# A graph layer on one core: VectorE's masks and one-hots made one slot ahead, with other ring sizes

## The chip, the core and the metric

One core of a Trainium2 chip. The metric is the device time of one execution in microseconds; the kernel before takes 1254.35 us (median of 3 runs, 1250.93 to 1255.43). Smaller is better.

## What is computed

One layer of a graph network over 6250 nodes of 128 features and 200000 edges that are sorted by their destination:

```python
h = relu(layernorm(x))
H = gelu(h @ W1.T + b1)                       # 6250 x 128
T = gelu(H @ WA.T) @ WB.T                     # 6250 x 4, the mix weights of a node
agg = gelu(segment_sum(H[src][:, :, None] * T[src][:, None, :], dst))   # 6250 x 128 x 4
cnt, sT = segment_sum(1, dst), segment_sum(T[src], dst)
node = einsum('nhm,nm->nh', agg, sT) / max(cnt, 1)
out = x + gelu(concat([node, H])) @ W2.T + b2
```

The destinations are drawn unevenly: the low-numbered nodes have most of the edges.

## The kernel before

The sum over the edges is done in two ways side by side.

*Gathered part (nodes from 1536 on).* 796 tiles of 128 edges, in 398 groups of two. For each tile GpSimd gathers the 128 source rows (128 features, 4 mix weights and their bf16 parts) from `node_table` in HBM into a `ring` of 10 rows of tiles, one indirect DMA a tile (line 778, in program order, held at line 777 until the group that last used the ring slot is summed). VectorE makes a mask for the group: `make_eq` (L1158, two groups at a time) compares the destinations with 24 consecutive nodes, `make_mask` (L1170) multiplies with the four mix weights. TensorE sums the group with four matmuls over the masks and two over `eq` (`sum_group`, L1518 and L1521) into one of two pairs of PSUM halves; VectorE adds the result into the accumulator at a column that it reads into a register (`add_group`, L1182).

*Dense part (nodes up to 1535).* For these the kernel counts how often each source node sends to each destination node, and multiplies the count matrix with the products. The destinations fall into six chunks, treated one after the other from the last; a chunk's counts are made while the chunk before is multiplied. Per tile of edges ScalarE makes a one-hot of the source's low bits (L894 and L897, four tiles in a batch, two batches), VectorE a one-hot of the rest (`hots`, L1204, 294 to 490 columns, in `hot_a` with 6 buffers), and TensorE multiplies them (L1546). One to four tiles are a count group; its sum lies in one of two PSUM banks, and VectorE adds it into the count matrix (`add_counts`, L1195). The multiplication has 49 units a chunk, one for each 128 source nodes: 12 matmuls with the counts (L1565) and two or four for the sums (L1570). Each unit needs a 388 KB slice of `product_parts` from HBM, loaded by SyncE (L599) into one of 4 buffers (`cbuf`).

*Order.* Python lays out a list of slots ahead of time, `SLOTS`: 50 slots in stage 0, in which the `product_parts` are made (two slots for each pair of node tiles: L914 and L953 on ScalarE, L1325 and L1333 on VectorE, L588 the store), and 49 in each of the stages 1 to 5, one for each unit. A slot holds some groups of gathers and some count groups:

```
stage                      0    1    2    3    4    5
groups of gathers         50   52   76   78   78   64
count groups              76   50   81   92  112    0
tiles counted             76  100  210  228  234    0
slots with 3 count groups  0    0    0    4   24    0
```

Every engine walks the same list. TensorE does in each slot the sums of the slot's gathers, then its counts, then the unit. VectorE does for each group its mask, and after every second one the additions of the two groups before; then for each count group the one-hots and after them the addition of the count group before (`pending_c`), and in stage 0 its part of the products. At a stage's end ScalarE moves four PSUM banks out (`evacuate`, L903 and L905), and VectorE reads a maximum from what it moved (L1286). In stage 5 VectorE also checks counts and bounds, and SyncE loads some large arrays (`own_part`, `dense_columns`) in the same queue as the `product_parts`. A prologue of 84 us (the node table) comes before, and a tail of 58 us (the output) after.

What holds what back: a mask waits for its two gathers, and for the mask buffer of four groups before. A one-hot waits until the tile of `HA` before is counted. A group's sum waits for its mask, and the first of each pair for the additions of the pair before the last. A count group waits for its one-hots on both sides, and for the addition of the count group two before. A `product_parts` load waits for the end of the unit `CB` before.

## Time and profile before

```
median without a profile      1254.35 us (1250.93 to 1255.43)
span of the profiled run      1435.7 us
VectorE busy                   915.1 us (64%)
TensorE matmul busy           1168.7 us (81%)
GpSimd busy                    849.4 us (59%), nearly all gathers
ScalarE busy                   635.0 us (44%)
TensorE's granted clock        0.847 of full speed on average
```

All rows and durations below are from the one profiled execution. Its span is 181 us longer than the median of the runs without a profile, so a sum that is made in it has to be carried over. A granted clock of 1 means TensorE's level of 2.4 GHz all the time, 0.5 that of 1.2 GHz. The busy time of TensorE counts pipelined matmuls with modelled ends, so it isn't work alone. In the rows of waits, "issue" is idle time for which the profile shows no releaser, and "remote" a releaser that it has no record of; some matmul records are missing.

### The profile page before, as it was taken

The numbers are of one execution on the slowest core, as the hardware profiler recorded it, in microseconds if no ns is written. First come the engines' busy times: TensorE is split into PE (matmuls) and PEld (weight loads), VectorE is DVE, ScalarE is ACT, GpSimd is POOL, SyncE is SP. The second block draws the span as 40 slices with busy tenths as digits, with TensorE's granted clock in tenths as the row PEclk, the third lists the DMA queues.
The fourth block names the chain that finished last, engine by engine and source line by source line (L and its number), as shares of the span: only waits on it lengthen the run. The fifth ranks groups of instructions, "written<-read, shape, count | busy, mean of one in ns | idle before, by whom it ended". The sixth has DMA issues, their size and how long they took to land.

```text
span 1435.7 us, 26415 instructions
## 1 busy us (share of the span) xinstructions
PE 1168.7 (81%) x7416; PEld 773.5 (54%) x7416; DVE 915.1 (64%) x2876; ACT 635.0 (44%) x1498; POOL 849.4 (59%) x910
## 2 busy tenths in 40 slices
PE   5948777688887888988788888777888878779888
PEld 3724333366665555656556556555556655456544
DVE  8569987746764677675567767466666755262256
ACT  6976656344342455453455555244554531000023
POOL 5457655556566666666656566655655666656526
PEclk9965555589999999899989999988888999889978
DMA  6345544466555445444545444444444446765523
GB/s 203 130 135 175 171 145 161 142 184 180 167 169 165 134 135 135 126 138 138 144 123 137 121 123 133 140 129 120 127 121 109 125 127 185 176 186 169 174 47 84
DMA packets 100422, 205.73 MB, mean 143 GB/s; under 512 B 29570, under 2 KB 48336, under 8 KB 99611
## 3 DMA queue, kind: packets, MB, share of 16 engines
q1 hardware_dynamic: 74804, 146.92, 33.9%
q0 software_dynamic: 25472, 57.11, 16.2%
q8 instruction: 62, 1.02, 0.3%
q14 instruction: 84, 0.69, 0.1%
HBM read 171.73 MB, written 32.22 MB: 142 GB/s over the span
## 4 chain that ended last, share of the span: by engine, by line
PE 56%; DVE 15%; issue 14%; another core or an unknown queue 5%; DVEq 4%; ACT 3%; POOL 2%; DMA 2%; SPq 0%; ACTq 0%; POOLq 0%
PE ps L1565 23%; PE ps L1546 12%; PE ps L1518 12%; PE ps L1521 3%; DVE big L1195 3%; DVE big L1325 3%; DVE mask L1170 2%; PE ps L1570 2%; DVE q L1204 2%; DVEq L1152 2%; DVE big L1182 2%; POOL q L778 1%; DMA q<-node_table,src_g 1%; PE ps L1614 1%
## 5 line engine op out<-in xcount | busy, mean ns | idle before, releaser
L778 POOL DMA_INDIRECT q<-node_table,src_g x796 | 778.1, 977 | 497.1 <-PE ps L1521 218.6
L1565 PE MATMUL ps<-big,q 128*128 128x298 bf16 (+2 forms) x2940 | 522.7, 319 | 21.1 <-issue 14.2
L894 ACT ACTIVATE hot_b<-iota_b,q 128x128 bf16<-128x128 bf16 x848 | 270.0, 389 | 420.3 <-PE ps L1546 329.4
L1518 PE MATMUL ps<-mask,q 128*128 128x96 f32 x1592 | 291.2, 311 | 107.0 <-DVE mask L1170 67.8
L1565 PEld LDWEIGHTS ps<-big,q 128*128 128x128 bf16 x2940 | 286.5, 105 | 123.7 <-issue 31.1
L1195 DVE TENSOR_TENSOR big<-big,ps 128x294 f32 (+2 forms) x411 | 226.5, 551 | 186.4 <-PE ps L1546 125.6
L1518 PEld LDWEIGHTS ps<-mask,q 128*128 128x128 f32 x1592 | 244.9, 216 | 184.7 <-DVE mask L1170 118.3
L1546 PE MATMUL ps<-q,hot_b 128*128 128x294 bf16 (+2 forms) x848 | 221.7, 349 | 101.0 <-issue 58.4
L1204 DVE TENSOR_SCALAR q<-iota_a,q 128x294 bf16<-128x294 f16 (+2 forms) x848 | 238.0, 324 | 35.4 <-issue 19.8
L1170 DVE TENSOR_TENSOR mask<-eq,q 128x192 f32<-128x192 bf16 x398 | 141.9, 357 | 74.5 <-issue 40.0
L1182 DVE TENSOR_TENSOR big<-big,ps 128x120 f32 x398 | 110.2, 277 | 123.2 <-remote 53.0
L1546 PEld LDWEIGHTS ps<-q,hot_b 128*128 128x128 bf16 x848 | 73.7, 99 | 190.5 <-issue 85.6
L897 ACT ACTIVATE hot_b<-hot_b,ones 128x512 bf16<-128x512 bf16 x212 | 153.0, 722 | 6.9
L1570 PE MATMUL ps<-big,q 128*128 128x149 bf16 (+2 forms) x588 | 138.6, 236 | 3.2 <-issue 3.2
L1521 PE MATMUL ps<-eq,q 128*13 128x24 bf16 x796 | 82.4, 177 | 4.3 <-issue 4.3
L903 ACT ACTIVATE big<-ps 128x400 f32<-128x400 f32 x4 | 1.9, 484 | 188.9 <-PE ps L1565 188.9
L1570 PEld LDWEIGHTS ps<-big,q 128*128 128x128 bf16 x588 | 62.3, 106 | 40.8 <-issue 12.9
L1526 PE MATMUL ps<-zero 128*128 128x512 bf16 x126 | 69.7, 634 | 0.0
L914 ACT ACTIVATE big<-big 128x128 bf16<-128x128 f32 x196 | 59.7, 388 | 13.8 <-DMA big<-node_table 13.5
L1521 PEld LDWEIGHTS ps<-eq,q 128*13 128x13 bf16 x796 | 39.1, 88 | 46.8 <-issue 17.0
L1158 DVE TENSOR_TENSOR eq<-iota_b,dloc_g 128x96 bf16<-128x96 bf16 x199 | 51.1, 257 | 13.1 <-issue 3.3
L811 POOL TENSOR_TENSOR big<-big 128x1024 f32<-128x1024 f32 (+1 forms) x13 | 32.7, 2522 | 37.3 <-DVE big L1444 37.0
(145 smaller groups left out, 665.7 us busy)
## 6 DMA issues: line engine op xcount, KB each, us to landing
q<-product_parts SPq DMA_DIRECT2D x245, 388.0 KB
product_parts<-big SPq DMA_DIRECT2D x24, 776.0 KB
q<-node_table,src_g POOLq DMA_INDIRECT x796
node_table<-big SPq DMA_DIRECT2D x12, 280.0 KB, 3.0
big<-node_table SPq DMA_DIRECT2D x24, 140.0 KB
own_part<-big SPq DMA_DIRECT2D x12, 256.0 KB, 3.0
out_dram<-q SPq DMA_DIRECT2D x12, 256.0 KB, 2.0
big<-own_part SPq DMA_DIRECT2D x2, 1024.0 KB, 6.2
```

Source lines behind the costliest of these rows:

```text
L778: pool.indirect_dma_start(out=ring[:, t % R, :], out_offset=None, in_=table, in_offset=bass.IndirectOffsetOnAxis(ap=src_g[:, t:t + 1], axi ...
L894: last = nc.scalar.activation(hot_b[:, b % 2, i, :], iota_b[:, :], ACT.Abs, bias=nkey_b[:, t:t + 1])
L897: nc.scalar.activation(hot_b[:, b % 2, 0:n, :], hot_b[:, b % 2, 0:n, :], ACT.Relu, bias=ones[:, :], scale=-1.0).then_inc(hot_b_ready, 1)
L1170: nc.vector.tensor_tensor(mask[:, g % MB, :, :, :], eq[:, g % EB, :, None, :].to_broadcast([P, G, MIX, W]), ring[:, s:s + G, D:D + MIX][:, ...
L1182: nc.vector.tensor_tensor(to, to, group_psum(g, 0, SLOT) .rearrange("p (m w) -> p m w", w=W), ALU.add).then_inc(added, 1)
L1195: nc.vector.tensor_tensor(to, to, ps[:, 1 + c.number % 2, 0:NT * w].rearrange("p (a w) -> p a w", w=w), ALU.add).then_inc(counts_added, 1)
L1204: nc.vector.tensor_scalar(hot_a[:, ct % HA, 0:n], iota_a[:, 0:n], key_a[:, c.key + t:c.key + t + 1], None, ALU.is_equal).then_inc(hot_a_re ...
L1518: nc.tensor.matmul(o[:, 0:MIX * W], ring[:, s + t, 0:D], mask[:, b, t, :, :], start=(t == 0), stop=(t == G - 1))
L1521: last = nc.tensor.matmul(o[0:NP, MIX * W:SLOT], ring_b[:, s + t, TP:TP + NP], eq[:, e, t, :], start=(t == 0), stop=(t == G - 1))
L1546: nc.tensor.matmul(ps[:, 1 + c.number % 2, 0:n], hot_b[:, ct // HB % 2, ct % HB, :], hot_a[:, ct % HA, 0:n], start=(t == 0), stop=(t == c. ...
L1565: last = nc.tensor.matmul(ps[:, 3 + m, 0:n], c[:, LEAD + P * (MIX * part + m):LEAD + P * (MIX * part + m + 1)], counts[k % 2][:, a, c0:c1] ...
L1570: nc.tensor.matmul(ps[:, 3 + m, n:n + d1 - d0], c[:, 0:P], counts[k % 2][:, a, c0 + d0:c0 + d1], start=False, stop=False)
```

## The change

VectorE's loop over the slots is put in another order, and three sizes change.

- `prepare(slot)` is new. It does for every group of gathers of a slot the register load, `make_eq` and `make_mask`, and for every count group the wait for the keys, the register load and `hots`. It is called for the first slot ahead of the loop, and in each slot for the next one.
- In slot i, after `prepare(SLOTS[i + 1])`, come the additions of slot i: of gathers in pairs as soon as two are there, of all its count groups. `pending_c` is gone.
- VectorE's registers for start columns become 8 and 8 (6 and 4 before).
- `R`, the ring of gathers, 12 for 10; `HA`, VectorE's one-hot buffers, 8 for 6; `CB`, the `product_parts` buffers, 3 for 4.

No instruction on any engine is added or left out. The orders on TensorE, ScalarE, GpSimd and SyncE stay.

```diff
-R = 10
+R = 12
-HA = 6
+HA = 8
-CB = 4
+CB = 3
-        QW = 3104 + R * ROW + CTT + ...
+        QW = CB * CROW // 2 + R * ROW + CTT + ...
+            def prepare(slot):
+                for g in slot.gathers:
+                    starts_g[g] = column(regs_g[g % 8], base_g[:, g:g + 1], N - D0)
+                    if g % 2 == 1 and g + 1 < NG:
+                        make_eq(g + 1)
+                    make_mask(g)
+                for c in slot.counts:
+                    if c.index == 0:
+                        v.wait_ge(keys_ready, KEYED[c.chunk])
+                    cell = GROUP0[c.chunk] + c.index
+                    starts_c[c.number] = column(regs_c[c.number % 8], base_c[:, cell:cell + 1],
+                                                WIDE[c.chunk] - CWS[c.chunk])
+                    hots(c)
+
             make_eq(0)
-            pending_g, pending_c = [], None
-            for slot in SLOTS:
+            pending_g = []
+            prepare(SLOTS[0])
+            for i, slot in enumerate(SLOTS):
...
-                for g in slot.gathers:
-                    starts_g[g] = column(regs_g[g % 6], base_g[:, g:g + 1], N - D0)
-                    if g % 2 == 1 and g + 1 < NG:
-                        make_eq(g + 1)
-                    make_mask(g)
-                    pending_g.append(g)
-                    if g % 2 == 1 and g >= 3:
-                        add_group(pending_g.pop(0))
-                        add_group(pending_g.pop(0))
+                if i + 1 < len(SLOTS):
+                    prepare(SLOTS[i + 1])
+                pending_g += slot.gathers
+                while len(pending_g) >= 2:
+                    add_group(pending_g.pop(0))
+                    add_group(pending_g.pop(0))
                 for c in slot.counts:
-                    if c.index == 0:
-                        v.wait_ge(keys_ready, KEYED[c.chunk])
-                    cell = GROUP0[c.chunk] + c.index
-                    starts_c[c.number] = column(regs_c[c.number % 4], ...)
-                    hots(c)
-                    if pending_c:
-                        add_counts(pending_c)
-                    pending_c = c
+                    add_counts(c)
...
-                if not slot.counts and pending_c:
-                    add_counts(pending_c)
-                    pending_c = None
```

## Rows read from the trace of the kernel before

**Rows 1.** The page: the span, and busy time of each engine.

```profile
span 1435.7 us, 26415 instructions
PE 1168.7 (81%) x7416; PEld 773.5 (54%) x7416; DVE 915.1 (64%) x2876; ACT 635.0 (44%) x1498; POOL 849.4 (59%) x910
```

**Rows 2.** Busy time by stretch: stages 2 to 4, 1, 0, 5; clock, DMA share, GB/s.

```profile
445.00:1175.00 730.00, 604.62 (x4122) 416.07 (x4122) 472.37 (x1561) 350.77 (x875) 443.95 (x465) 0.90 0.48 131
287.00:445.00 158.00, 134.12 (x1098) 103.91 (x1096) 98.14 (x293) 60.80 (x138) 94.10 (x100) 0.95 0.60 175
84.00:287.00 203.00, 147.01 (x508) 71.73 (x509) 165.63 (x528) 124.71 (x320) 124.41 (x113) 0.50 0.50 156
1175.00:1378.00 203.00, 173.96 (x1164) 112.70 (x1164) 80.75 (x237) 14.07 (x14) 117.95 (x126) 0.89 0.60 168
```

**Rows 3.** Waits of VectorE in stages 2 to 4: total us, times, longest.

```profile
DVE big L1195 <- PE ps L1546: 96.6, 74, 2.9
DVE big L1195 <- remote: 51.8, 20, 3.5
...
DVE big L1182 <- remote: 10.9, 3, 4.2
DVE smax L1286 <- ACT q L903: 10.5, 2, 6.1
...
DVE big L1182 <- PE ps L1521: 7.9, 7, 2.2
DVE smax L1286 <- ACT sstage L905: 4.1, 1, 4.1
```

**Rows 4.** Groups of instructions in stages 2 to 4: busy us, mean ns; idle before.

```profile
L778 POOL DMA_INDIRECT q<-node_table,src_g x465 | 444.0, 955 | 287.1 <-PE ps L1521 133.4 <-issue 103.2 <-remote 50.5
...
L1204 DVE TENSOR_SCALAR q<-iota_a,q 128x294 bf16<-128x294 f16 (+2 forms) x672 | 180.7, 318 | 15.9 <-issue 9.0
...
L1195 DVE TENSOR_TENSOR big<-big,ps 128x294 f32 (+2 forms) x285 | 157.0, 551 | 150.6 <-PE ps L1546 96.6 <-remote 51.8 <-issue 2.0
...
L1170 DVE TENSOR_TENSOR mask<-eq,q 128x192 f32<-128x192 bf16 x232 | 83.2, 358 | 23.0 <-issue 19.3 <-PE ps L1521 0.6 <-DVE eq L1158 0.6
...
L1182 DVE TENSOR_TENSOR big<-big,ps 128x120 f32 x232 | 64.1, 276 | 43.9 <-DVE big L1182 13.4 <-issue 11.7 <-remote 10.9
```

**Rows 5.** Waits of GpSimd and TensorE in stages 2 to 4.

```profile
POOL q L778 <- issue: 103.2, 336, 0.6
...
PE ps L1546 <- DVE big L1195: 24.4, 28, 2.9
...
PE ps L1518 <- DVE mask L1170: 15.9, 18, 2.3
```

**Rows 6.** Timeline, TensorE in one slot of stage 3 at full clock: start, duration.

```profile
834.93 0.58 PE L1518 MATMUL ps<-mask,q 128*128 128x96 f32 x4
...
835.58 1.02 PE L1546 MATMUL ps<-q,hot_b 128*128 128x294 bf16 x6
...
836.44 0.29 PE L1565 MATMUL ps<-big,q 128*128 128x298 bf16 x1
...
838.09 0.58 PE L1518 MATMUL ps<-mask,q 128*128 128x96 f32 x4
```

**Rows 7.** Timeline, a slot of stage 4: VectorE's addition, TensorE's third count group.

```profile
1104.51 0.46 DVE L1195 TENSOR_TENSOR big<-big,ps 128x294 f32 x1 [2.88 <-PE ps L1546]
...
1105.34 0.59 PE L1546 MATMUL ps<-q,hot_b 128*128 128x294 bf16 x2 [0.77 <-issue]
```

**Rows 8.** The chain before the first unit (start, us), and a DMA issue with landing.

```profile
282.81 4.01 DMA q<-product_parts
...
big<-own_part SPq DMA_DIRECT2D x2, 1024.0 KB, 6.2
```

**Rows 9.** Waits of VectorE in stage 5.

```profile
DVE mask L1170 <- DMA q<-node_table,src_g: 28.3, 13, 9.0
```

**Rows 10.** The gathers in stage 0: busy us, mean ns; idle before.

```profile
L778 POOL DMA_INDIRECT q<-node_table,src_g x112 | 124.4, 1111 | 81.1 <-PE ps L1521 51.2 <-issue 26.8 <-DMA own_part<-big 3.0
```

More of the change, by code:

```diff
@@ L217, in gnn_kernel @@
         assert MIX * D0 <= HALF and NT * D <= ACC0 - HALF
-        QW = 3104 + R * ROW + CTT + -(-CTT // 2) + HA * NT * CW // 2 + MIX * SW
+        QW = CB * CROW // 2 + R * ROW + CTT + -(-CTT // 2) + HA * NT * CW // 2 + MIX * SW
         q = sb("q", [P, QW])
@@ L1145, in _ @@
             v.wait_ge(consts, 7)
-            regs_g = [nc.vector.alloc_register(f"start_g{i}") for i in range(6)]
-            regs_c = [nc.vector.alloc_register(f"start_c{i}") for i in range(4)]
+            regs_g = [nc.vector.alloc_register(f"start_g{i}") for i in range(8)]
+            regs_c = [nc.vector.alloc_register(f"start_c{i}") for i in range(8)]
             starts_g, starts_c = {}, {}
@@ L1288, in _ @@
                 if s == S and slot.at % 2 == 0 and slot.at // 2 < NAB:
-                    i = slot.at // 2
+                    b = slot.at // 2
                     v.wait_ge(counts_added, CGG)
-                    nc.vector.tensor_reduce(most_p[:, i:i + 1], counts[1][:, AB * i:AB * i + AB, :], axis=AX.XY,
+                    nc.vector.tensor_reduce(most_p[:, b:b + 1], counts[1][:, AB * b:AB * b + AB, :], axis=AX.XY,
                                             op=ALU.max).then_inc(most_ready, 1)
@@ L1296, in _ @@
                         .then_inc(most_ready, 1)
-                for g in slot.gathers:
-                    starts_g[g] = column(regs_g[g % 6], base_g[:, g:g + 1], N - D0)
-                    if g % 2 == 1 and g + 1 < NG:
-                        make_eq(g + 1)
-                    make_mask(g)
-                    pending_g.append(g)
-                    if g % 2 == 1 and g >= 3:
-                        add_group(pending_g.pop(0))
-                        add_group(pending_g.pop(0))
-                for c in slot.counts:
-                    if c.index == 0:
-                        v.wait_ge(keys_ready, KEYED[c.chunk])
-                    cell = GROUP0[c.chunk] + c.index
-                    starts_c[c.number] = column(regs_c[c.number % 4], base_c[:, cell:cell + 1],
-                                                WIDE[c.chunk] - CWS[c.chunk])
-                    hots(c)
-                    if pending_c:
-                        add_counts(pending_c)
-                    pending_c = c
+                if i + 1 < len(SLOTS):
[4 more added lines that the diff above has]
+                    add_group(pending_g.pop(0))
+                for c in slot.counts:
+                    add_counts(c)
                 if s == 0 and slot.at % 2 == 0:
```

## The prediction, made before the changed kernel ran

> **What bounds the kernel now.** I read the spans of the stages first, then who VectorE waits for, then what one gather, one VectorE instruction and one piece of TensorE work cost. The profiled execution takes 1435.7 us and no engine fills it: TensorE 81%, VectorE 64%, GpSimd 59% [rows 1]. Cut at the ends of the five unit stages (each has 49 units of 12 L1565 matmuls), the three middle stages are one block of 730 us, 147 slots of 4.97 us, half of everything [rows 2]. I work on that block first.
>
> In the block VectorE is busy 472.4 us. It waits for other engines 96.6 + 51.8 + 10.9 + 10.5 + 7.9 + 4.1 = 181.8 us, 148.4 of them in `add_counts` (L1195) for the count matmuls; "remote" there is a count matmul whose record is missing, as the line waits for nothing else [rows 3]. The rest, 730 - 472.4 - 181.8 = 76 us, are register loads and the adds' own chain. So VectorE's work alone needs 472.4 + 76 = 548 us, 3.7 us a slot.
>
> GpSimd: a gather is busy 955 ns [rows 4] and its gap is 103.2/336 = 0.307 us where nothing holds it [rows 5]: 1.262 us. The block holds 465 of them: 587 us, 3.99 us a slot. The other 143 us it waits for ring slots.
>
> TensorE at the full clock: a group takes 835.58 - 834.93 = 0.65 us, a count matmul of 294 columns (836.44 - 835.58)/6 = 0.143, a unit 838.09 - 836.44 = 1.65 [rows 6]. 147 units, 232 groups and 672 count matmuls (114 of 490 and 140 of 392 columns, scaled by columns) come to 243 + 151 + 113 = 507 us. The granted clock is 0.90 in the block, a mix of the 1.2 and 2.4 GHz levels [rows 2]; at that mix 507/0.90 = 563 us.
>
> So three engines need 587, 563 and 548 us and together take 730. The lost 143 us are hand-overs. [rows 7] shows one: VectorE stands 2.88 us in front of an addition while TensorE finishes the unit before and the sums; only after that addition does it make the one-hots of the third count group, for which TensorE then idles 0.77 us. TensorE's idle time in the block under `add_counts` and the masks by name is 24.4 and 15.9 us [rows 5], and more stands as "issue".
>
> **The change, part by part.**
>
> *Masks and one-hots a slot ahead.* No VectorE instruction is added or removed; the order changes. When VectorE stands in front of an addition of slot i, the masks and one-hots of slot i+1 are made, so the wait costs TensorE nothing at the start of slot i+1. The preparation of an average slot is 1.58 masks x 0.358 + 4.57 one-hots x 0.318 = 2.0 us [rows 4], with its share of the 76 us of gaps 2.5. It runs beside TensorE's unit, sums and counts, 1.65 + 1.0 + 0.7 = 3.3 us, which covers it.
>
> *The added wait.* Queued behind the preparation are now the additions of slot i. Two count banks exist, so the third group of a slot needs the first one's addition. 28 slots of the block have three groups (24 of them in its last stage). Cost at most: preparation, two group additions (0.55) and one count addition (0.55) uncovered, 28 x 3.6 = 101 us; at least nothing, a gain being excluded, as this wait is there before in a shorter form. I take one round trip of 0.65 us on VectorE each, 18 us, because the 3.3 us cover the 2.5; VectorE then needs 566, still under the gathers' 587. `prepare` can itself stand still: for a gather not landed, or for a free one-hot buffer. Then the additions stand behind it, and TensorE behind them.
>
> *Ring of 12, one-hots 8.* One more group of two gathers may be under way, which makes up for the masks being wanted about 1.6 groups earlier. Neither changes a duration. With 8 one-hot buffers the last one-hots of slot i+1 (two average slots hold 9.1) need the first counts of slot i done: in step with TensorE, no stall. From nothing to a small gain; taken as nothing, inside the block's term.
>
> *Three product_parts buffers.* A load is then issued when the unit three before has ended, so it has two slots, not three. The nearest row lands in 4.01 us; a 1 MB load ahead of it in the same queue takes 6.2 us more [rows 8], together 10.2 against two slots of 8.6 and the sums before the unit. Some six bulk transfers of the last stage stand in this queue. Between 0 and 6 x 1.6 = 10 us; taken as 3, since slots at the stage's pace usually cover it.
>
> *The block.* It can't go under 587. I add the stage changes as they stand (10.5 + 4.1 = 15 us [rows 3]) and 28 us for what two engines near their limit (587 and 566) lose when a slot with two gathers meets one with three count groups; that last is my guess between 0 and the 128 us that are left. 587 + 15 + 28 = 630: 100 us saved.
>
> *The other stages* [rows 2]. The first unit stage, 158 us, TensorE busy 134: of the 24 idle I take 8. The last, 203 us: VectorE waits 28.3 us for gathers [rows 9], against which the sixth ring group helps; 7. The product stage before them, 203 us, is VectorE's own work (165.6 busy) and its order hardly changes: 3, from -5 to 10. The prologue and the 58 us after the units don't change.
>
> **The sum.** 1435.7 - 100 - 8 - 7 - 3 + 3 = 1320.7 us for the profiled span. The median without a profile, 1254.35, is 0.874 of 1435.7, and nothing in the trace says which instructions are shorter there. All by one factor: 1320.7 x 0.874 = 1154. If the 1.262 us of a gather don't shrink at all, the block now takes 730 x 0.874 = 638 and can't go below 587 + 43 x 0.874 = 625; that saves 13, the rest 15 x 0.874 = 13: 1228. Neither end has a row that is nearer, so I take a gather that shrinks by half the factor, 550 us: 550 + 38 = 588, saving 50 + 13: **1191 us**.
>
> **The rivals.**
> - *The gather pace is fixed*: 1228 us. For it: it is the largest floor of the block. Against: GpSimd stands 143 us in the block for the ring.
> - *Everything shrinks alike*: 1154 us.
> - *VectorE isn't really ahead*: each preparation waits for its gathers or one-hot buffers, the additions wait behind it, and the time stays 1254 us. For it: in the last stage masks already wait for gathers [rows 9]. Against: in the block the masks wait for none.
> - *The loads starve TensorE* (slower): with three buffers three slots can't take less than the landing L and one unit (about 1.65 us). At the landing of 4.01 us that is 1.9 us a slot and binds nothing. It decides from L about 11.7 us in all stages; at L = 12, with units of 1.4, 1.65 and 2.2 us by their columns, the unit stages take 219, 669 and 232 us, the span 1462 and the time 1277 us. For it: the 6.2 us of bulk loads and a DMA share of 0.60 in the first and last stages. Against: one wait for such a load, 2.9 us at the very first, in the whole trace.
> - *Bunched one-hots hold up the gathers* (slower): if GpSimd stood still while VectorE makes one-hots, a slot would need 3.99 + 4.57 x 0.318 = 5.4 us for its gathers, the block 800 us and the whole 1302 us. For it: in the product stage, where VectorE runs long tensor operations, gathers take 1111 ns [rows 10]. Against: in the block, with 672 one-hots among them, 955 [rows 4].
>
> Of the last one the Trainium skill has a rule (SBUF — State Buffer, its part on the engine side and the "DVE blocks DMA" trap): while VectorE runs an operation in a two-port mode, GpSimd can't write the descriptors of its DMAs. By that rule one-hots in such a mode would cost the gathers their whole length; the block's rows speak against it for these, the product stage's row for it there.
>
> **How the numbers follow.** Forecast 0.36; fixed gather pace 0.25; everything alike 0.17; not ahead 0.10; starved loads 0.10; one-hots against gathers 0.02. About 0.5% is what a measurement of this kernel can tell from no change. Faster: 0.36 + 0.25 + 0.17 = 0.78; same 0.10; slower 0.12. The range runs from just under the 1154 of the scaled sum to past the 1228 of the fixed pace, which leaves out the last three cases: 1150 to 1245 us.
>
> **What would show it.** VectorE's wait in `add_counts` falls from 148 us in the block to under 70; TensorE's wait for masks there goes to nearly nothing; GpSimd's wait for the sums falls from 184 us (133.4 + 50.5 [rows 4]) to under 60 and its gathers follow at 1.26 us; the granted clock of the block rises above 0.90; the middle stages take about 210 us each. Wrong: TensorE waits for `product_parts` more than a few us, or for `add_counts` much longer in the stage with three groups a slot; or the block in the profile shrinks as said and the median doesn't follow.

## The result, and the profile after

The changed kernel takes 1276.39 us (median of 4 runs, 1265.98 to 1277.18) where the kernel before takes 1253.96 us (4 runs): a ratio of 1.017, 95% interval 1.012 to 1.022, so it is slower by some 22 us. The forecast was 1191 us, and the whole range, 1150 to 1245, lay on the other side.

One thing has to be known before any row is read. The runs of this study fall into sessions in which the kernel before takes 1247 to 1260 us, and sessions in which it takes 1434 to 1466 us. The times above and the profile after come from the first kind; the profile of 1435.7 us from which I predicted is of the second. I call them session A (about 1254) and session B (1434 and more). The expectations below speak of two kinds of chip; that is the same thing under a name that proved wrong, since one chip number (12) gave both. Each ratio below is against runs of before on the same chip in the same session. Profiles are compared within a kind only, unless the text says otherwise, and often come from two sessions of that kind.

So the profile to lay beside the changed kernel's is not that of [rows 1], but one of the kernel before in session A. The run b_copy3 is that: the kernel before, unchanged, 1250.39 us, span 1248.7.

> The kernel before, once more, for a profile that stands beside this call's runs. On a quick chip 1254 us and stage 4 between 205 and 225 us (then the changed kernel's 241 us there carries its loss); on a slow one 1435 to 1455 us with stage 4 at 253.

Busy time by stretch, one line for each of stages 0 to 5, cut at the first evacuation that ends each (columns as in [rows 2]: stretch, length, busy us of TensorE, its weight loads, VectorE, ScalarE and GpSimd, granted clock, DMA share, GB/s). First the kernel before (b_copy3):

```profile
84.00:288.00 204.00, 146.95 (x507) 71.54 (x507) 165.40 (x528) 126.07 (x320) 125.14 (x113) 0.50 0.50 155
288.00:419.30 131.30, 125.37 (x1094) 102.49 (x1095) 95.19 (x293) 60.90 (x138) 94.67 (x99) 0.97 0.74 212
419.30:609.80 190.50, 178.13 (x1354) 126.68 (x1352) 151.93 (x492) 112.40 (x278) 144.36 (x152) 0.99 0.60 165
609.80:811.90 202.10, 183.34 (x1385) 130.83 (x1384) 157.21 (x526) 120.91 (x298) 151.18 (x158) 0.97 0.58 158
811.90:1009.30 197.40, 177.96 (x1391) 129.16 (x1390) 158.25 (x543) 116.85 (x297) 149.17 (x157) 1.00 0.58 160
1009.30:1191.90 182.60, 161.22 (x1169) 106.29 (x1168) 80.17 (x237) 14.29 (x13) 118.86 (x128) 0.94 0.68 188
```

Then the changed kernel, its span first:

```profile
span 1275.0 us, 26415 instructions
...
84.00:266.50 182.50, 129.32 (x508) 71.84 (x509) 160.74 (x524) 123.53 (x320) 118.38 (x114) 0.58 0.56 173
266.50:391.80 125.30, 123.26 (x1094) 101.25 (x1095) 99.14 (x298) 60.66 (x137) 92.47 (x96) 0.99 0.77 217
391.80:584.60 192.80, 178.05 (x1355) 128.97 (x1355) 156.86 (x493) 112.57 (x279) 146.16 (x153) 0.98 0.59 164
584.60:794.70 210.10, 184.21 (x1384) 135.08 (x1383) 163.02 (x526) 121.06 (x298) 150.34 (x158) 0.95 0.56 152
794.70:1035.80 241.10, 190.42 (x1391) 142.81 (x1390) 165.99 (x541) 117.98 (x298) 148.17 (x156) 0.89 0.49 131
1035.80:1217.30 181.50, 160.46 (x1169) 106.73 (x1168) 82.15 (x236) 14.29 (x13) 117.78 (x126) 0.94 0.70 190
```

The second number of each line is what to read. (Stage 4 of b_copy3 is shorter than expected, 197.4 us for 205 to 225.) Stage by stage the change does -21.5, -6.0, +2.3, +8.0, +43.7 and -1.1 us; together +25.4, against 26.3 between the spans. Two things follow at once. The loss sits in stage 4, the one with 24 slots of three count groups, where TensorE's clock falls from 1.00 to 0.89; stage 3, with four such slots, loses 8.0 us, and stage 2, with none, 2.3. And there is a gain, which sits in the product stage, where I had looked for 3 us.

The third thing is in the first fence alone: stages 2 to 4 of the kernel before take 190.5 + 202.1 + 197.4 = 590.0 us in session A, not the 730 of [rows 2]. The floor that I had worked out for the gathers was 587. What GpSimd and VectorE wait for there (columns as in [rows 3]), b_copy3 from 419.3 to 1009.3:

```profile
POOL q L778 <- issue: 130.5, 428, 0.4
DVE big L1195 <- PE ps L1546: 25.4, 40, 2.5
...
POOL q L778 <- PE ps L1521: 15.1, 37, 1.9
```

In the same stages of session B GpSimd stood 133.4 + 50.5 us behind TensorE's sums and VectorE 96.6 + 51.8 us in its additions [rows 3, 4]; here it is 15.1 and 25.4. A gather costs 444.7/465 = 0.956 us (GpSimd's busy time on L778 in this stretch) and a gap of 130.5/428 = 0.305, 1.261 together, just as in session B [rows 4, 5], and 465 of them make 586 us of the 590.

What went wrong in stage 4 shows in one slot of the changed kernel (start, duration, operation, idle before it and its releaser):

```profile
905.05 0.67 PE L1547 MATMUL ps<-q,hot_b 128*128 128x294 bf16 x2 [2.94 <-DVE big L1195]
...
906.76 2.19 PE L1566 MATMUL ps<-big,q 128*128 128x298 bf16 x8
906.91 0.51 DVE L1204 TENSOR_SCALAR q<-iota_a,q 128x294 bf16<-128x294 f16 x2
...
910.17 0.94 POOL L778 DMA_INDIRECT q<-node_table,src_g  x1 [4.74 <-PE ps L1522]
...
911.07 0.67 PE L1547 MATMUL ps<-q,hot_b 128*128 128x294 bf16 x4
911.40 1.11 DVE L1204 TENSOR_SCALAR q<-iota_a,q 128x294 bf16<-128x294 f16 x4 [3.99 <-PE ps L1547]
...
912.43 0.26 DVE L1182 TENSOR_TENSOR big<-big,ps 128x120 f32 x1
...
912.90 0.28 DVE L1182 TENSOR_TENSOR big<-big,ps 128x120 f32 x1 [0.21 <-DVE big L1182]
913.12 0.46 DVE L1195 TENSOR_TENSOR big<-big,ps 128x294 f32 x1
913.63 0.42 PE L1547 MATMUL ps<-q,hot_b 128*128 128x294 bf16 x2 [1.89 <-DVE big L1195]
```

Follow VectorE. It has made two one-hots of the next slot by 907.4 and then stands 3.99 us: the eight one-hot buffers are full, and one comes free only when TensorE counts a tile of this slot, after the unit of the slot before and this slot's sums. At 911.40 it goes on with four one-hots, 1.11 us, then two group additions, 0.69, then the first count addition at 913.12. TensorE's third count group needs just that addition and starts at 913.63, after 1.89 us of idling (2.94 in the slot before). Here each waits for the other once in the slot; I call this the lockstep. And TensorE can pay a second time: after 2.94 us idle its unit's last eight matmuls take 2.19 us, the 1.2 GHz level; at the 2.4 GHz level they take 1.18. In this stage 47 units show their last eight matmuls as one row of the timeline, and for 12 of them it takes 1.85 us or more; in b_copy3 for none of 46. Meanwhile GpSimd waits 4.74 us for a ring slot. By the Trainium skill (TensorE: Matmul & The Clock Gate, "HAM oscillation — how this bites in real kernels") TensorE falls back to the low clock after idling and starts the next piece of work cold; this trace agrees, with the two matmuls at 905.05 taking 0.67 us where those at 913.63 take 0.42, and with 0.89 in this stage against 1.00 before. Summed over the stage, 794.7 to 1035.8:

```profile
POOL q L778 <- PE ps L1522: 54.5, 29, 4.8
PE ps L1547 <- DVE big L1195: 46.8, 24, 3.7
...
DVE q L1204 <- PE ps L1547: 28.9, 24, 4.0
```

That is 24 waits of TensorE and 24 of VectorE in a stage that has 24 slots with three count groups. Of TensorE's, 23 stand before the last count group of a slot, right ahead of the unit; VectorE's are not tied to these slots one by one. The same three waits in stage 4 of the kernel before (b_copy3, 811.9 to 1009.3) are 4.0, 9.3 and under 1 us:

```profile
PE ps L1546 <- DVE big L1195: 9.3, 19, 0.9
...
POOL q L778 <- PE ps L1521: 4.0, 11, 0.9
```

### The profile page after: what moved, and what is told of

It is laid out like the page before. It is cut to its first block, busy times and chain, and to the rows that moved or that the text cites. A ratio compares the mean times of both kernels' runs of the same rounds, so it can differ in the third digit from the quotient of the medians.

```text
span 1275.0 us, 26415 instructions
## 1 busy us (share of the span) xinstructions
PE 1070.0 (84%) x7416; PEld 753.7 (59%) x7416; DVE 925.6 (73%) x2876; ACT 634.3 (50%) x1498; POOL 843.3 (66%) x910
## 4 chain that ended last, share of the span: by engine, by line
PE 33%; DVE 26%; issue 14%; POOL 11%; DVEq 6%; ACT 5%; DMA 5%; SPq 0%; ACTq 0%; POOLq 0%
PE ps L1566 16%; POOL q L778 11%; DVE big L1195 7%; DVE q L1204 7%; PE ps L1519 7%; PE ps L1547 5%; DVE mask L1170 3%; DMA q<-node_table,src_g 3%; DVEq L1152 2%; DVE big L1329 2%; DVE big L1182 2%; PE ps L1522 2%; PE ps L1571 1%; ACT big L821 1%; ACT hot_b L894 1%
## 5 line engine op out<-in xcount | busy, mean ns | idle before, releaser
L778 POOL DMA_INDIRECT q<-node_table,src_g x796 | 771.9, 970 | 344.7 <-issue 210.1
L1566 PE MATMUL ps<-big,q 128*128 128x298 bf16 (+2 forms) x2940 | 484.8, 305 | 6.2 <-DMA q<-product_parts 5.4
L1519 PE MATMUL ps<-mask,q 128*128 128x96 f32 x1592 | 275.0, 300 | 71.7 <-DVE mask L1170 70.1
L1566 PEld LDWEIGHTS ps<-big,q 128*128 128x128 bf16 x2940 | 273.8, 101 | 97.1 <-DMA q<-product_parts 5.6
L1519 PEld LDWEIGHTS ps<-mask,q 128*128 128x128 f32 x1592 | 239.0, 211 | 121.8 <-DVE mask L1170 105.5
L1547 PE MATMUL ps<-q,hot_b 128*128 128x294 bf16 (+2 forms) x848 | 200.8, 338 | 93.6 <-DVE big L1195 79.5
L1195 DVE TENSOR_TENSOR big<-big,ps 128x294 f32 (+2 forms) x411 | 230.4, 561 | 49.9 <-DVE big L1195 38.8
L1204 DVE TENSOR_SCALAR q<-iota_a,q 128x294 bf16<-128x294 f16 (+2 forms) x848 | 224.1, 321 | 50.1 <-PE ps L1547 36.6
L1182 DVE TENSOR_TENSOR big<-big,ps 128x120 f32 x398 | 109.3, 275 | 88.6 <-PE ps L1522 46.0
L1571 PE MATMUL ps<-big,q 128*128 128x149 bf16 (+2 forms) x588 | 133.0, 226 | 0.0
L1522 PE MATMUL ps<-eq,q 128*13 128x24 bf16 x796 | 81.8, 177 | 0.0
L1571 PEld LDWEIGHTS ps<-big,q 128*128 128x128 bf16 x588 | 59.2, 101 | 31.1 <-issue 2.2
L1527 PE MATMUL ps<-zero 128*128 128x512 bf16 x126 | 63.7, 583 | 0.0
```

Of the source, the lines that this page charges most:

```text
L778: pool.indirect_dma_start(out=ring[:, t % R, :], out_offset=None, in_=table, in_offset=bass.IndirectOffsetOnAxis(ap=src_g[:, t:t + 1], axi ...
L1182: nc.vector.tensor_tensor(to, to, group_psum(g, 0, SLOT) .rearrange("p (m w) -> p m w", w=W), ALU.add).then_inc(added, 1)
L1195: nc.vector.tensor_tensor(to, to, ps[:, 1 + c.number % 2, 0:NT * w].rearrange("p (a w) -> p a w", w=w), ALU.add).then_inc(counts_added, 1)
L1204: nc.vector.tensor_scalar(hot_a[:, ct % HA, 0:n], iota_a[:, 0:n], key_a[:, c.key + t:c.key + t + 1], None, ALU.is_equal).then_inc(hot_a_re ...
L1519: nc.tensor.matmul(o[:, 0:MIX * W], ring[:, s + t, 0:D], mask[:, b, t, :, :], start=(t == 0), stop=(t == G - 1))
L1522: last = nc.tensor.matmul(o[0:NP, MIX * W:SLOT], ring_b[:, s + t, TP:TP + NP], eq[:, e, t, :], start=(t == 0), stop=(t == G - 1))
```

## The experiments

### The sizes alone

Order of before, with `R = 12`, `HA = 8` and `CB = 3`; the registers stay 6 and 4, as that order needs no more. With it, in the same session, the kernel before once more with a profile.

> The kernel before once more, for a second profile. The profile that the prediction was made from spans 1435.7 us where the runs without one take 1254; the changed kernel's profile spans 1275, as its runs do. If the first profile was an odd execution, this one spans about 1252 us, and its stages 2 to 4 take 620 to 640 us, not 730; then the hand-over losses that I counted were mostly of that execution. If the kernel before is always slowed by being profiled, it spans about 1430 again.

> VectorE's order of before with the changed sizes (12 gathers, 8 one-hots, 3 parts buffers). If the new order costs the time (the one-hots of the next slot wait for counts of this slot and stand ahead of its first addition), this takes 1245 to 1258 us, that is no slower than before, and the changed kernel is 20 us or more behind it. If the three parts buffers cost it (TensorE waits for loads), this takes 1270 us or more.

Both ran in session B: b_copy 1452.79 us (not for being profiled, since the 19 runs of before beside it take 1451 to 1465), sizes_only 1457.72, which is 1.0008 of before (0.998 to 1.004). A second session B gave the same:

> The order of before with the sizes of after (ring 12, one-hots 8, parts 3). Theory (sizes do nothing): 0.997 to 1.003 of before, each of stages 0 to 5 within 3 us of before's. Rival (three parts buffers or the memory's other layout cost time that the order hides): over 1.005, with TensorE's waits for product_parts over 5 us in stages 1 to 5.

1460.81 us, 1.002 (0.9998 to 1.0041). Stages 0 and 1 end at 449.4 us in sizes_only and at 448.0 in b_copy. So the sizes by themselves do nothing that can be measured, there; three `product_parts` buffers starve nobody. The expected times of sizes_only were those of session A and can't be judged here. In the changed kernel TensorE waits for such a load once, 5.4 us at the very first unit, 2.9 before. In session A the sizes were not run alone; but the run woven2 below has the same sizes there and is faster than before, so by themselves they can't be what makes the changed kernel slower.

### Half of the order

```diff
# masks_ahead: prepare() makes masks only; counts as before
                 for c in slot.counts:
+                    one_hots(c)
                     if pending_c:
                         add_counts(pending_c)
                     pending_c = c
# hots_ahead: prepare() makes one-hots only; masks and
# group additions as before, then prepare(SLOTS[i + 1])
                 for c in slot.counts:
                     add_counts(c)
# adds_first: masks ahead, all additions, then the one-hots ahead
                 for c in slot.counts:
                     add_counts(c)
+                for c in SLOTS[i + 1].counts: one_hots(c)
```

> The changed kernel with only the masks made a slot ahead; one-hots and count additions in the order of before (one-hots of a group, then the addition of the group before). Theory of the loop: stage 4 falls from 241 us to 205 to 225 us, the whole to 1230 to 1255. If masks a slot ahead are the harm (they wait for gathers that land late), this is as slow as the changed kernel, 1270 us or more, with over 50 us of VectorE's waits on gathers.

> The changed kernel with only the one-hots made a slot ahead; masks and group additions in the order of before. Theory of the loop (one-hots that wait for counts stand ahead of the addition TensorE waits for): stage 4 stays slow, near its time in the changed kernel, and the whole within 1% of the changed kernel. Theory that the masks ahead are the harm: 1.5% or more faster than the changed kernel.

> The changed kernel, but in each slot VectorE makes only the masks of the next slot ahead; then the additions of this slot, and after them the one-hots of the next. The third count group of a slot is then held up by no one-hot. Theory of the loop (one-hots that wait for TensorE's counts stand ahead of the addition that TensorE waits for): stage 4 falls from 241 us to under 215, the whole to 1225 to 1250 us. Theory that the masks' wait for gathers holds the additions: stage 4 stays near 240 us and the whole near 1275, since the masks still stand ahead of the additions.

All in session B, where the changed kernel itself, run as a_copy, takes 1441.82 us, 1.002 of before (0.999 to 1.005):

> The kernel before, once more. In the run of b_copy this same program took 1452.8 us where it had taken 1254 elsewhere, so whole executions of it differ by 16% between chips. If this call's chip is of the quick kind: 1254 us, and stages 2 to 4 take 610 to 640 us instead of the 730 of the rows that the prediction used. If it is of the slow kind: 1450 us again.

> The changed kernel beside the kernel before, on this call's chip. On a quick chip 1.7% slower than before (1276 against 1254). On a slow chip, if what is slow there is a hand-over between engines, of which the new order takes some away, it is 1 to 6% faster than before (1370 to 1440 us against 1455); if the slowness is something that the order doesn't touch, 1 to 3% slower there too.

masks_ahead takes 1619.99 us, 1.112 (1.106 to 1.117); hots_ahead 1513.62, 1.052 (1.048 to 1.057); adds_first 1465.6, 1.005 (1.002 to 1.008). The theory had expected masks_ahead and adds_first to be faster than the changed kernel and hots_ahead within 1% of it: none of the three came out so, and neither branch of a_copy's expectation did. Either half alone is much worse than both or none, in session B; in A they were not run. For the first, one row stands out (VectorE's waits in stages 2 to 4 of masks_ahead):

```profile
DVE big L1182 <- PE ps L1529: 294.8, 115, 6.0
```

The group additions of slot i now stand ahead of that slot's own one-hots. VectorE waits 295 us for sums that TensorE makes only after the unit of the slot before, and by the order the counts that come next find no one-hots: TensorE stands 176.3 us before them, though the profile lists that as "issue" and not under the one-hots. In hots_ahead it is the mask: TensorE waits 72.6 us for it in 70 places, and the one-hots that stand before it wait 88.6 us for buffers. In adds_first TensorE still waits 79.7 us for count additions (12.8 in b_copy2), and VectorE 56.0 + 81.8 us in the group additions ahead of them. What these runs suggest is that it matters what an addition is placed behind, and what is placed behind an addition, more than that something is made "ahead"; they don't separate it from what makes session B slow.

### The one-hots' memory

The first suspect of the lockstep were the one-hot buffers, which I had costed at nothing. They are cut for 490 columns; in stage 4 a tile needs 294. hot_flat is the changed kernel with the same memory handed out by the width that a tile needs, so 12 to 13 tiles fit (TensorE reads them at the same places).

```diff
-                    if ct >= HA:
-                        v.wait_ge(counted, ct - HA + 1)
-                    nc.vector.tensor_scalar(hot_a[:, ct % HA, 0:n], ...)
+                    if HOT_AFTER[ct]:
+                        v.wait_ge(counted, HOT_AFTER[ct])
+                    nc.vector.tensor_scalar(hot_a[:, HOT_AT[ct][0]:HOT_AT[ct][1]], ...)
```

> The changed kernel with its order as it is, but the memory of the 8 one-hot buffers handed out by width: 12 or 13 one-hots fit in stage 4 (294 columns each), 9 to 11 in stages 2 and 3. In stage 4 a next slot's one-hot then hardly ever waits for a count of this slot. Theory of the loop: VectorE's wait in front of the one-hots there goes to near zero, and stage 4 gets 8 to 25 us shorter, the whole 1 to 2% shorter than the changed kernel; what stays is that the whole preparation stands ahead of the first addition. If that standing ahead alone costs stage 4 its time, and not the buffers, this changes less than 0.4%.

Session A: 1255.62 us, 1.0017 of before (0.9988 to 1.0046). Stage 4 and TensorE's longest wait in it:

```profile
794.80:1018.50 223.70, 182.44 (x1390) 137.93 (x1390) 166.17 (x541) 117.81 (x297) 148.52 (x156) 0.92 0.52 141
...
PE ps L1560 <- DVE big L1208: 41.0, 26, 3.4
```

Stage 4 falls from 241.1 to 223.7, as expected, so the buffers were 17 of its 44 us; VectorE's wait for a free one-hot buffer falls from 28.9 us to 0.3. But TensorE still waits 41.0 us in 26 places for the count addition. That is the other part: the one-hots and group additions that stand before it.

### Additions woven in

woven takes away most of what stands there: masks are made a slot ahead as in the change, but the one-hots of slot i+1 come one group at a time, between the count additions of slot i.

```diff
                 for c in slot.counts:
                     add_counts(c)
+                    if ahead:
+                        one_hots(ahead.pop(0))
+                for c in ahead:
+                    one_hots(c)
```

> Masks of the next slot, group additions of this one, then turn by turn one count addition of this slot and the one-hots of one count group of the next. Every addition of a count then waits for at most one group's one-hots. Theory of the loop: faster than the changed kernel by 2 to 5%, most of it in stage 4 (three count groups in a slot). Rival, that each addition in front of one-hots makes VectorE wait for TensorE (as in the run adds_first): within 1% of adds_first, which was 0.5% slower than before.

> As before: masks a slot ahead, then one count addition of this slot and the one-hots of one group of the next turn by turn. It was 0.7% faster than before on a slow chip. If what differs there is only a slower hand-over, it is 1 to 3% faster than before on a quick chip, and again 0.7% on a slow one.

> The woven order with the one-hot memory by width. By the theory of the loop the weaving has already taken the one-hots from in front of the additions, so that the extra buffers give at most 0.5% more; if buffers are what binds, 1.5% or more beyond woven.

In session B woven takes 1428.85 us, 0.993 of before (0.991 to 0.996). In session A the same kernel (woven2) takes 1231.32 us, 0.981 (0.977 to 0.985), and with the memory by width (woven_flat) 1227.74, 0.978 (0.974 to 0.982): it beats both kernels. The expectation for session A, 1 to 3% faster than before, held, and so did that for the extra buffers, at most 0.5% more; in B woven is 0.9% faster than the changed kernel, where 2 to 5% was expected. Stages 2 to 4 of woven2:

```profile
397.20:585.70 188.50, 176.45 (x1355) 127.96 (x1354) 149.25 (x491) 112.35 (x278) 143.09 (x150) 0.99 0.61 166
585.70:785.50 199.80, 181.03 (x1386) 133.94 (x1384) 152.44 (x528) 120.82 (x299) 152.27 (x157) 0.96 0.59 160
785.50:986.50 201.00, 171.70 (x1390) 131.15 (x1389) 153.76 (x542) 117.49 (x297) 150.87 (x159) 0.98 0.57 158
```

Stage 4 is back at 201 us, with its clock at 0.98. But the three stages take 589.3 us, where before takes 590.0: the better order repairs the lockstep and gains nothing more. Its gain over before is the 22 us that the first evacuation comes earlier (397.2 against 419.3).

### What binds stages 2 to 4

586 us of gathers against 590, and an order that doesn't move it, is an agreement of numbers. To test it, b_half leaves out the second gather of each group, and a_half is the changed kernel with the same left out. The mask and the sums of the second tile use the first one's row; every other instruction stays, and the result is another one.

```diff
             for t in range(TG):
...
+                if t % G:
+                    continue
                 pool.indirect_dma_start(out=ring[:, t % R, :], ...)
...
-                nc.tensor.matmul(o[:, 0:MIX * W], ring[:, s + t, 0:D], mask[:, b, t, :, :], ...)
+                nc.tensor.matmul(o[:, 0:MIX * W], ring[:, s, 0:D], mask[:, b, t, :, :], ...)
```

> The kernel before with half of its gathers left out: of each group only the first tile is gathered, and the second uses its row again, so the sums of the gathered part are other ones; every other instruction stays. Theory (on the chip of 1254 us the gathers' own pace binds stages 2 to 4: 465 x 1.262 = 587 us of 590): the three stages together fall to between 530 and 570 us, what VectorE (548) and TensorE (507 at the full clock) need; the run is 25 to 60 us shorter. Rival (the hand-overs between TensorE and VectorE bind there, and the gathers only follow): the three stages stay within 10 us of 590. On a chip where before takes 1435 us and more, where the gathers stand 143 us for the ring, the first predicts under 20 us of change in these stages.

> The changed kernel with the same half of its gathers left out. Theory (stage 4 is set by the lockstep: one-hots of the next slot, then the additions, then TensorE's third count group): stages 2 and 3, 193 and 210 us, fall by 10 to 30 us each, and stage 4 stays at 225 us or more of its 241. Rival (the gathers, late by the ring, make the length of stage 4): stage 4 falls below 210 us.

> The kernel before with half of its gathers left out, again. On a chip where before takes about 1254 us: if the gathers' pace (465 x 1.262 = 587 us) is what holds stages 2 to 4 at 590 us, they fall to 550 to 570 us, since the same kernel needed 569.5 us on a chip where before took 1458; if the hand-overs hold them, they stay over 580. On a chip of the other kind: 1211 us again within 1%, and the three stages at 570.

b_half2 in session A takes 1212.84 us, 0.967 (0.957 to 0.977); b_half in session B 1211.13 us, 0.830 (0.825 to 0.834). Stages 2 to 4 in one stretch, b_half2 and then b_half:

```profile
419.50:987.90 568.40, 528.91 (x4124) 384.84 (x4124) 459.58 (x1561) 349.83 (x873) 222.43 (x233) 1.00 0.51 138
```

```profile
417.30:986.80 569.50, 529.95 (x4124) 385.89 (x4123) 459.22 (x1561) 349.80 (x874) 221.52 (x233) 0.99 0.51 138
```

In session A the stages fall from 590.0 to 568.4. So the gathers' pace did hold them, and right below it, 22 us down, something else does; by the sums of the prediction that is VectorE and TensorE. With the gathers as they are, an order of VectorE could gain no more there than the 4 us between 586 and 590. In session B the first expectation for these stages, under 20 us of change, is refuted: they fall from 726 (b_copy2) to 569.5. More on that in the last section.

a_half (session B, 1227.13 us, 0.841) settles stage 4. Its stages 2, 3 and 4:

```profile
390.60:572.10 181.50, 173.85 (x1353) 127.54 (x1353) 154.25 (x493) 112.39 (x279) 72.37 (x77) 1.00 0.54 143
572.10:772.60 200.50, 182.06 (x1385) 134.69 (x1384) 159.13 (x528) 120.82 (x299) 74.71 (x78) 0.96 0.49 131
772.60:1001.00 228.40, 183.74 (x1391) 138.22 (x1389) 163.83 (x541) 117.95 (x298) 73.96 (x78) 0.93 0.42 114
```

Stage 4 takes 228.4 us with half the gathers; in b_half it took 192.6. The order costs 36 us there with half of the gathers gone, and TensorE still waits 30.7 us for count additions, so the 54.5 us that GpSimd waits in the changed kernel's stage 4 are a result of the lockstep and not its cause.

### Gathers moved to the product stage

```diff
-GATHERS = [50, 52, 76, 78, 78, 64]
+GATHERS = [60, 52, 74, 75, 74, 63]
```

> Woven order with one-hot memory handed out by width, and the groups of gathers spread 60, 52, 74, 75, 74, 63 over the stages (50, 52, 76, 78, 78, 64 before): stage 0, which VectorE and ScalarE set, takes ten groups from stages 2 to 4 and 5. Theory (each gather costs 1.262 us in stages 2 to 4 and nothing in stage 0): nine groups less in stages 2 to 4 are 18 gathers or 23 us, of which stage 0 gives back up to 10 x (0.36 + 0.28) = 6 us of VectorE's: 5 to 17 us faster than the same kernel with the old spread (1228 us where before takes 1254). Rival (hand-overs bind all stages): no gain, or 5 us slower by stage 0.

Session B only: 1433.04 us, 0.982 (0.978 to 0.986), where woven, with neither the memory by width nor this spread, was 0.993 in another session B. Stages 2 to 4 take 721.5 us (731.0 in woven), stage 5 202.7 (207.8), but stages 0 and 1 end 15 us later, at 449.3. The two effects aren't separated, so the expected 5 to 17 us can't be judged, and that ten groups cost 15 us in stage 0, where up to 6 were expected, speaks against more of it.

## Why the prediction was wrong

**The base.** The first step that failed is the one that gave the block 143 us to lose. I read that from a trace of 1435.7 us and carried it over to 1254 by one factor, with nothing in the trace that said which instructions are shorter. The two that I compared aren't: a gather is 0.956 us here and 0.955 there, a one-hot 0.317 and 0.318. What is shorter is idle time, and TensorE's work at the higher clock. Of the 181 us between the span and the median, 140 lie in the block (730 against 590): they were nearly the whole of the 143 us that I meant to save. The forecast took a gather that shrinks by half the factor; it doesn't shrink at all. With the block at 590 and a floor of 587, the gain there is at most 3 us. The rival with the fixed pace had the mechanism right. It gave 1228 us by a sum that still took 638 us for the block; that woven2 and woven_flat land at 1231 and 1228 is therefore chance, since their gain is in the product stage. The starved loads' 1277 us at L = 12 lies within 1 us of the measured time, and that is chance too: TensorE waits for one load in the whole trace, for 5.4 us.

**The hand-overs.** The base alone doesn't excuse the forecast, for in session B, where the 143 us do exist, the change saves none of them either: a_copy takes 745.5 us for the block, b_copy2 726.1. The step that failed there is that VectorE's wait before an addition "costs TensorE nothing" once the next slot's preparation is made. The wait in `add_counts` does fall, from 103.0 + 44.1 us in b_copy2 to 11.6 + 3.1. But it comes back in other places (a_copy, 429.7 to 1175.2):

```profile
PE ps L1547 <- DVE big L1195: 86.1, 52, 4.8
...
DVE q L1204 <- PE ps L1547: 55.5, 41, 3.8
DVE q L1204 <- remote: 46.5, 37, 3.7
```

TensorE's wait for that addition is 12.8 us in b_copy2, and a wait of VectorE for a free one-hot buffer isn't among its rows there. GpSimd stands 118.6 + 87.4 us for the ring, 140.7 + 44.0 in b_copy2.

**The third count group.** Priced at 18 us, from 0 to 101, and then put under the gathers' floor as if it cost nothing there. I took it from the spare time of an average slot (2.5 us of preparation beneath 3.3 us of cover). But it is paid in slots that aren't average: in stage 4 about every second slot has three count groups with six tiles (one has eight), and one or two groups of gathers. Stage 2 tells the same from the other side: most neighbouring slots hold eight to twelve tiles there too, but never in three groups, and it loses 2.3 us. Measured: stage 4 +43.7 us and stage 3 +8.0, of which the 46.8 - 9.3 = 37.5 us more waiting of TensorE in stage 4 and its lower clock are the visible parts. With the buffers' part in it, it is 43.7/24 = 1.8 us a slot, half of the 3.6 that I had as the upper bound a slot. The row was there: [rows 7] shows VectorE's wait before an addition and TensorE's third group behind it in just such a slot of stage 4. And the reason given for the lower bound, that "this wait is there before in a shorter form", said nothing of its new length.

**The one-hot buffers.** "In step with TensorE, no stall" was the sentence. Two neighbouring slots of stage 4 hold ten to twelve tiles in nearly all cases, against eight buffers, so VectorE stands up to 3.99 us in front of the ninth, and the additions stand behind it. hot_flat measures 17 us. Both terms are one mechanism: VectorE waits for counts with one-hots queued, and TensorE waits for an addition behind them. The rival that the additions wait behind a preparation that can't proceed named this, but it said that the time would stay; it ends slower. No rival of mine had the slower side from this cause.

**The product stage.** Predicted -3, measured -21.5. (With stage 1 it is -27.5; in session B the two stages together end 20 us earlier, 429.7 against 449.7.) I had argued that VectorE's own work fills it. It is busy 165.4 of 204.0 us before and 160.7 of 182.5 after, so what shrank is 17 us of its gaps and 5 of its work. One example from b_copy3:

```profile
259.53 0.39 DVE L1204 TENSOR_SCALAR q<-iota_a,q 128x294 bf16<-128x294 f16 x1 [0.62 <-issue]
259.84 0.40 DVE L1195 TENSOR_TENSOR big<-big,ps 128x294 f32 x1
260.81 0.37 DVE L1204 TENSOR_SCALAR q<-iota_a,q 128x294 bf16<-128x294 f16 x1 [0.57 <-PE ps L1546]
```

With one or two one-hots at a time and TensorE at the low clock, a count group of before can cost a short round trip of 0.6 us; in the changed order they are made together, a slot ahead. But VectorE's named waits of this kind, 7.8 + 4.9 us up to 266 us, are less than the gain. The kernels with the gain (changed, hot_flat, woven) have both the masks and the one-hots ahead; adds_first has both too, and ends stages 0 and 1 only 5 us before b_copy; sizes_only has no gain. TensorE's granted clock in the stage rises as well, from 0.50 to 0.58, and its busy time falls from 147.0 to 129.3 us; whether that is a cause of the gain or comes of it no run tells. The cause of this gain stays open.

**The rest.** Stage 1: -8 predicted, -6.0 measured. Stage 5: -7 and -1.1; its masks wait less for gathers there (45.5 us, 66.1 in b_copy3), but the group additions more for sums (21.7 us, 5.2), and the stage is no shorter. Three parts buffers: 3 us, measured one wait longer by 2.5 us. The starved loads and the one-hots that hold up gathers are both refuted: no later wait for a load, and a gather of 0.95 us in stage 4 with 234 one-hots around it.

**Of what would show it**, much came true on paper and meant nothing: against the rows of session B the block shrank from 730 to 644 us (630 was forecast), its clock rose from 0.90 to 0.94 and VectorE's wait in `add_counts` fell under 3 us. But before in session A has 590 us, 0.99 and 25.4 us. That was one of the signs named for a wrong prediction, a block that shrinks in the profile with a median that doesn't follow. The other is TensorE's wait for `add_counts` in the stage with three groups a slot, which grew. GpSimd's wait for the sums, 74.0 us, missed its bound of 60.

## What to carry to other kernels

Before summing in a trace, see that its span is near the median that has to be predicted. Where they differ by 14%, the idle time that one hopes to save may be the difference itself, and the floor of the busiest engine (here 587 us against 590) has to be compared with the time that really counts.

On an engine that works in order, work made ahead is placed in front of something. Price it in the densest slots and not in the average one: there the price is every instruction ahead of the first result that another engine waits for, plus whatever those instructions themselves wait for. If it must be ahead, weave it between the results.

## What the hardware showed that I had not expected

The same program on the same inputs took 1253 to 1254 us or 1438 to 1458 (medians), with a spread of 1.1% at most within a session. The difference is gone when half of the gathers is left out (1212.84 and 1211.13 us, stages 2 to 4 568.4 and 569.5). Engine durations agree in both. What differs is TensorE: in stages 2 to 4 of b_copy2 (session B) it stands still with nothing in the profile that holds it, and its clock is 0.89 for 0.99:

```profile
PE ps L1546 <- issue: 46.0, 69, 3.9
PE ps L1518 <- issue: 29.8, 38, 2.4
```

The same two rows are 5.4 us and none in b_copy3, and 9.3 us and none in b_half. One such place in b_copy2:

```profile
1073.11 0.87 PE L1546 MATMUL ps<-q,hot_b 128*128 128x294 bf16 x4
...
1073.71 0.94 POOL L778 DMA_INDIRECT q<-node_table,src_g  x1 [0.30 <-issue]
1074.96 0.94 POOL L778 DMA_INDIRECT q<-node_table,src_g  x1 [0.30 <-issue]
1076.21 0.94 POOL L778 DMA_INDIRECT q<-node_table,src_g  x1 [0.30 <-issue]
1077.06 0.46 DVE L1195 TENSOR_TENSOR big<-big,ps 128x294 f32 x1 [3.45 <-remote]
...
1077.89 0.41 PE L1546 MATMUL ps<-q,hot_b 128*128 128x294 bf16 x1 [3.91 <-issue]
```

VectorE and TensorE both stand for over 3 us, and a matmul between them has no record, while GpSimd issues one gather after the other. Some 76 us of such standing and the lower clock (the 507 us of work that I had estimated, at 0.89 for 0.99, is 58 us more) come near the 136 us by which the stages differ. What a gather does to TensorE in a session B, and why not in a session A, stays open. The run that should have told traffic from the indirect form fell into a session A:

```diff
+                if t % G:
+                    pool.dma_start(ring[:, t % R, :], table[r0:r0 + P, :]).then_inc(gathered[t % R], 16)
+                    continue
                 pool.indirect_dma_start(out=ring[:, t % R, :], ...)
```

> The kernel before in which each group's second gather is a plain copy of 128 neighbouring rows of node_table (the same 71 KB into the same ring row, still issued by GpSimd), so the sums of the gathered part are other ones. On a chip where before takes 1435 us and more, TensorE idles there 46 + 30 us in stages 2 to 4 with nothing in the profile that holds it, and 9 us with half the gathers left out. If the traffic of the second gather causes that (its bytes, its packets, the ring going round), it stays: over 50 us, and the run stays over 1380 us. If GpSimd's work on the list of rows (the indirect form) causes it, it falls under 25 us and the run lies near the 1211 us of half the gathers, at most 1280. On the other kind of chip: the stages 2 to 4 within 15 us of their 590, or less where a plain copy costs GpSimd less than 1.26 us.

It takes 1215.38 us, 0.969 (0.960 to 0.979), and says nothing about B. But it shows what the pace of A is made of. Its stages 2 to 4 in one stretch, and the plain copies in them as a group (columns as in [rows 4]):

```profile
415.80:988.50 572.70, 529.73 (x4125) 383.76 (x4125) 464.62 (x1561) 350.09 (x874) 365.41 (x464) 1.00 0.60 166
```

```profile
L780 POOL DMA_DIRECT2D q<-node_table x232 | 134.6, 580 | 0.7 <-issue 0.6
```

A plain copy of the same 71 KB keeps GpSimd for 580 ns with hardly a gap, an indirect one for 956 and a gap of 305. With half of them plain the bytes are all moved and the stages still fall by 17 us, where up to 15 were expected, or more if a plain copy costs GpSimd less: it is GpSimd's time for a gather that bound them, not the bytes. The plain copies read neighbouring rows, so what reading scattered rows costs by itself isn't separated.
